# POOL issues the gathers of a group in two parts, with a wait for the first part's landing between them

## The reference: what is computed

```
h = relu(layernorm(x))
Q, K, V = h@Wq+bq, h@Wk+bk, h@Wv+bv                  # 8 heads of 16
scores = sum(Q[dst]*K[src], -1)*scale + edge@We + be
p = exp(scores - segment_max[dst]) / segment_sum[dst]
x = x + segment_sum(p * V[src], dst) @ Wo + bo        # layer 0
h = logmap0(relu(layernorm(x))) @ W.T + b
x = x + expmap0(segment_sum(h[src]*dinv[src]*dinv[dst], dst))   # layer 1
```

## Time and profile before

| | |
|---|---|
| median of 3 runs | 1495.47 us |
| the profiled execution | 1495.77 us |
| its span, first to last instruction | 1493.8 us |
| mean granted TensorE clock | 0.678 of full speed |
| busy: PE, DVE, ACT, POOL | 946.3, 740.5, 391.2, 595.5 us |
| gathers of the first loop (L662) | 416, mean 953 ns |
| gathers of the second loop (L695) | 208, mean 955 ns |

### The profile page before, as it was taken

One profiled execution on the slowest core, in us unless ns is written; L12 is line 12 of the kernel. 1 busy time (PEld: TensorE's weight loads), 2 busy tenths in 40 slices (PEclk: granted clock), 3 DMA queues, 4 the chain that ended last, 5 costly groups with the idle time before them and its releaser, 6 DMA issues.

```text
span 1493.8 us, 22198 instructions
## 1 busy us (share of the span) xinstructions
PE 946.3 (63%) x5820; PEld 805.1 (54%) x5820; DVE 740.5 (50%) x2771; ACT 391.2 (26%) x1107; POOL 595.5 (40%) x629
## 2 busy tenths in 40 slices
PE   5355775775775775675675676733757756765775
PEld 2244664664664564564564565622656645654665
DVE  8344544544554554553553553583534544454454
ACT  1502212212212212211311311142323423432341
POOL 0544454354354354354354354005343443444341
PEclk9655566566566566566566566675867877877787
DMA  5622232232232232233232233012011111111111
GB/s 150 178 80 83 87 104 82 84 104 83 81 106 86 77 110 86 72 111 89 71 112 89 70 110 93 6 47 87 26 41 34 40 40 37 37 40 40 33 41 29
DMA packets 87848, 111.23 MB, mean 74 GB/s; under 512 B 20787, under 2 KB 65791, under 8 KB 87807
## 3 DMA queue, kind: packets, MB, share of 16 engines
q0 software_dynamic: 26624, 68.20, 15.8%
q1 hardware_dynamic: 61191, 42.64, 9.9%
HBM read 99.83 MB, written 10.95 MB: 74 GB/s over the span
## 4 chain that ended last, share of the span: by engine, by line
PE 33%; DVE 24%; issue 20%; another core or an unknown queue 19%; DVEq 2%; DMA 1%; SPq 0%; ACT 0%
PE ps_q L1547 10%; PE ps_q L1673 3%; PE ps_q L1698 3%; PE ps_s L1673 3%; PE ps_c L1531 3%; DVE sc L933 2%; DVE wv L1275 2%; PE ps_f L1601 2%; PE ps_f L1600 1%; DVE fwd_reset L1274 1%; DVE prod L927 1%; PE ps_c L1527 1%; DVE oh_lo L897 1%; PE ps_b L1673 1%
## 5 line engine op out<-in xcount | busy, mean ns | idle before, releaser
L662 POOL DMA_INDIRECT kv<-kv_tab,idx x416 | 396.6, 953 | 533.8 <-DVE wv L1004 367.6
L695 POOL DMA_INDIRECT kv<-hs_tab,idx x208 | 198.6, 955 | 335.9 <-PE ps_q L1682 191.6
L1369 ACT ACTIVATE S<-iota,nloc 128x128 f32<-128x128 f32 x384 | 122.0, 389 | 636.1 <-remote 635.0
L1547 PE MATMUL ps_q<-qwin,ST 128*128 128x128 f32 x832 | 207.0, 432 | 19.5 <-DVE prod L927 10.5
L1547 PEld LDWEIGHTS ps_q<-qwin,ST 128*128 128x128 f32 x832 | 187.1, 331 | 20.8 <-DVE prod L927 10.8
L1580 PE MATMUL ps_f<-oh_lo,oh_hi 128*50 128x64 bf16 x416 | 83.4, 301 | 96.2 <-issue 96.0
L927 DVE TENSOR_TENSOR prod<-kv,ps_q 128x512 f32<-128x512 f32 (+1 forms) x128 | 74.6, 583 | 140.2 <-issue 58.8
L1011 DVE TENSOR_SCALAR fb<-ps_c 128x8 f32<-128x8 f32 x32 | 5.3, 166 | 274.3 <-remote 267.3
L1559 PE MATMUL ps_r<-wv,S 128*128 128x137 f32 x832 | 140.1, 341 | 1.8 <-DVE wv L1004 1.8
L1559 PEld LDWEIGHTS ps_r<-wv,S 128*128 128x128 f32 x832 | 140.0, 253 | 2.1 <-DVE wv L1004 2.1
L1580 PEld LDWEIGHTS ps_f<-oh_lo,oh_hi 128*50 128x50 bf16 x416 | 54.2, 172 | 110.4 <-issue 109.4
(11 more groups left out here) (257 smaller groups left out, 1715.6 us busy)
## 6 DMA issues: line engine op xcount, KB each, us to landing
dloc_b<-dloc_tab SPq DMA_DIRECT2D x32, 416.0 KB
kv<-kv_tab,idx POOLq DMA_INDIRECT x416
attr_s<-in_attr SPq DMA_DIRECT2D x32, 192.0 KB
kv<-hs_tab,idx POOLq DMA_INDIRECT x208
kv_tab<-qkv SPq DMA_DIRECT2D x5, 640.0 KB, 4.0
x_tab<-x SPq DMA_DIRECT2D x32, 64.5 KB, 1.7
qwin<-q_tab SPq DMA_DIRECT2D x32, 64.0 KB
xwin<-in_x SPq DMA_DIRECT2D x32, 64.0 KB
```

Source lines behind the costliest of these rows:

```text
L662: pool.indirect_dma_start(out=kv[:, b, t, :], out_offset=None, in_=kv_tab, in_offset=bass.IndirectOffsetOnAxis(ap=idx[:, b, t:t + 1], axis ...
L695: pool.indirect_dma_start(out=kv[:, j, t, 0:D], out_offset=None, in_=hs_tab, in_offset=bass.IndirectOffsetOnAxis(ap=idx[:, j, t:t + 1], ax ...
L1369: A.activation(S[:, b, t, :], iota[:], ACT.Abs, bias=nloc[:, g, t:t + 1] if known(g) else nloc[:, bass.ds(g, 1), t:t + 1].rearrange("p g t ...
L1547: mm = M.matmul(ps_q[c % 2][:, (t - t0) * D:(t - t0 + 1) * D], ST[:, b, t, :], qwin[:, b, :], start=True, stop=True)
```

## The change

A constant `HALF = 7` is added. Before it issues the eighth gather of a group (`t == HALF`), POOL waits for gathers of the same group. In the first loop it waits on the semaphore of chunk 1 until the gathers of tiles 4, 5 and 6 have landed (`16 * (t - t0)` = 48 above what the earlier groups in that buffer left). In the second it waits until seven gathers on `s_g1[j]` have landed (112 above). Then it issues the other six.

```diff
+HALF = 7
...
                     for t in range(t0, t1):
+                        if t == HALF:
+                            wait_apart(pool, s_kv[b][c], 32 * (g - b) + 16 * (t - t0), (s_tab[0], 32 * 3))
                         pool.indirect_dma_start(out=kv[:, b, t, :], out_offset=None, in_=kv_tab,
...
                 for t in range(T):
+                    if t == HALF:
+                        wait_apart(pool, s_g1[j], 8 * T * (n - j) + 16 * t, (s_tab[0], 32 * 3))
                     pool.indirect_dma_start(out=kv[:, j, t, 0:D], out_offset=None, in_=hs_tab,
```

## The result

On the chip of the first comparison the change makes the kernel faster: 1228.81 us, the median of 4 runs (1227.59 to 1230.84), against 1495.45 us (1494.24 to 1497.34, 4 runs) before. The ratio is 0.8218, with a 95% interval of 0.8206 to 0.8231. The forecast was 1250 us. The profiled execution took 1227.9 us, of which 1225.7 is the span.

What follows compares the result with a forecast made beforehand. Bound: PE's completions held back while a burst of gathers runs. First loop 189, second loop 42 and heads 15 us sum to 246; 1495.8 - 246 gives about 1250 us, 1155 to 1320 for this case, stated range 1150 to 1420.

Steps and rivals of the forecast that it cites:

- What bounds the kernel: Both loops: gathers following one another delay PE's completions, from 6 to 10 us after a burst's first until it landed.
- The pause: POOL before each group's eighth gather: waiting for the landing takes 3 us, hidden while a period is over 19 us.
- First loop: L1011 released 7.6 us earlier, 1.3 lost again: 6.3 us a step, 30 steps, 189 us (bounds 228 and 111).
- the second burst's delay: First loop, the six gathers after the pause: completions may be delayed again up to 3.9 us; 1.3 us taken.
- Heads: Start of each loop, two groups gathered without a gap: last release sooner, 4.5 us each, together 15 us (0 to 25).
- Second loop: PE freed at the seventh gather's landing: 6.3, 2.7 us or nothing a pair; 3 taken, 14 pairs, 42 us (0 to 88).
- Blocks again at once: Rival, chance 0.20: second burst delays at once; first loop keeps about half, second gains nothing, about 1390 us.
- Nothing is freed: Rival, chance 0.14: the delay ends only when the thirteenth gather landed; 44 pauses of 3 us add 132 us, 1628 us.
- The delay only coincides with gathers: Rival, chance 0.05: something that gathers don't cause makes the delay; POOL's idle time takes in the pause, no change, 1495.5 us.

Runs made afterwards that it cites:

- the run without a pause on chip 9: The change with both added waits set on counts reached long before, so POOL does not stop, against the kernel before: 1508.74 us against 1510.69.

## Why the prediction was right, and what it did not see

**What bounds the kernel: right where it was read.** A delay of PE's completions while gathers follow one another, which a pause for a landing shortens, is what the traces with and without a pause show, on the first chip and on chip 9, and the run without a pause on chip 9 rules the instructions out. The conclusion was too narrow in one thing and too strict in another: DVE's completions are delayed too, and in the second loop some come through before the burst has landed. Nor is it shown that it is the landing, and not the stop, that frees them. The rule set against it in the prediction, *the Trainium skill's ("SBUF — State Buffer", "Who interferes with whom") that PE and ACT wait on nobody*, would not have foretold the traces of the chips with the delay, where PE idles 1.05 us and more between matmuls beside gathers, and agrees with chips 5 and 7. That section is about ports; whether a port has any part in the delay no run shows. The other, *issue a DMA early and wait for it late ("DMA: Bandwidth & Descriptors", "Rules for kernel authors")*, is right on chip 5 by 42 us and wrong on chip 9 by 244.

**The pause: 3 us taken, 2.5 and 2.3 us measured**, within the bounds 1.5 and 3.5. POOL resumes later than DVE by 0.9 us in the first loop, near the 1 us that was added for it.

**First loop: 189 us forecast, 213.8 measured** (from the first `weigh` to the last, 864.9 before and 651.1 after). The mis-sized term is the second burst's delay. It was put at 1.3 us a step, to make a period of 21.9; the period is 20.8 to 20.9. POOL has no idle time left, so six gathers of one group and seven of the next run on without a wait, and the delay does return (L1016 up to 2.0 us after L1572, not 0.42). But the pause then comes once every 20.9 us and ends 1.3 to 3.0 us behind L1572's start, in all steps but the first, so that little can be held back. One gather of each such run is also held up by `weigh` (2.31 us from 400.52); whether that break helps as well no run shows. (The working has the second burst end at 427.4 us; its own terms give 427.2, which changes nothing.) POOL's idle of about 2 us between groups was not there on the first chip (0.30 us); on chip 9 it is 1.3 to 2.5 us in 20 waits and 4.5 to 9.0 in five. There the loop gains 194.9 us (871.0 against 676.1), near the 189.

**Heads: 4.5 us forecast for the first, 15.6 measured** (first `weigh` at 97.4 before, 81.8 after). The estimate counted one release, moved from the twenty-sixth gather to the twentieth. The trace before also had a first wait of 9.00 us there, ahead of the 11.95 of the earlier trace rows, and both went. The rows shown left out the first of the two.

**Second loop: 42 us and a part of the heads (10.5) forecast, 38.8 measured** from the first gather to the end (477.2 against 438.4); on chip 9 it is 41.9 (484.1 against 442.2). The working was right in its times: throttled 5.7 us after the first gather, free at the seventh's landing, throttled again in the second burst. Taken apart, the head gives 8.8 us (first L1698 50.4 us after the first gather before, 41.6 after), the 14 pairs 31.6, or 2.3 a pair where 3 were taken, and the last stretch loses 1.6. That 3 came so near is partly luck: the working gave 6.3, 2.7 or nothing, according to where the delay falls, and 3 was chosen among them. The second pause shows what was behind it: 4.8 us a pair more (67.2 us over 14, on chip 9).

The terms give 213.8 + 15.6 + 38.8 = 268.2 us; the profiled executions differ by 267.9 (1495.77 - 1227.9). The forecast was 246. The prediction was read from a chip with the delay and measured on one; on chip 5 it would have had the sign wrong.

**The rivals.** "Blocks again at once" fell: the second burst leaves 5 us free. "Nothing is freed" fell: L1016 starts before the eighth gather. Its price, one pause times the number of groups for a loop that POOL bounds, came true on chips 5 and 7 in the second loop, 35 us. But its reason was another: on these chips there was nothing to free. "The delay only coincides with gathers" fell on the chips with the delay, since a pause among the gathers moves it.

**What was not seen** is that the delay does not come with the kernel alone. It was there on three chips and not on two, in every run of each visit. The prediction took the earlier trace rows as the behaviour of Trainium2. None of the views that it read told otherwise, but there was one hint: the releaser "another core or an unknown queue" for an engine of the same core. What makes two chips free of it and three not is open, and so is whether they stay so. The runs show no more than that the kernel, its order and the pace of the gathers are the same.

## What to carry to other kernels

Where an engine's wait for another ends on no known releaser while gathers run, look whether the releases fall on landings; if so, break the row of gathers with a wait for a landing; in the second loop a break after every four or five gathers did better than one in the middle. To place it just behind the completion on which most depends is an inference from the traces, and no run with the delay tested it. Measure such a change on several chips, with the kernel before beside it on each: here it is worth 16 to 18% on the two chips with the delay on which it was run (20% with a second pause in the second loop) and costs 4% on one without the delay. No version tried is best on both kinds of chip: with the delay it is the one with two pauses, without it the kernel before. And read before you add a pause how much the issuing engine idles a period: on chips 5 and 7 it cost little up to that idle time and nearly its full length beyond it.

## What the runs showed of the hardware that was not expected

- **Two kinds of chip, or of occasion.** The same kernel takes 1043 us on two chips and 1495 to 1511 us on three. On the slower ones completions of PE and DVE are held back, in the pairs shown from 5 to 6 us after the first gather of a burst: L1567's until 2.3 to 2.9 us after the last gather's end, others for 0.6 to 3.4 us. On the faster ones DVE follows 0.42 us after PE's L1572 starts, with gathers all around.
- **In the second loop the delay does not depend on the bytes of a row**: 4 and 512 bytes give 1505.93 and 1508.31 us, one run each.
- **POOL's wait for the landing of gathers takes 2.5 us for 1 KB rows and 2.3 us for 512 byte rows**, from the end of the last issue, on both kinds of chip. At the very first pause it is 4.6 us.
- **A gather issued beside `weigh` is held up until `weigh` ends.** Timeline of the change on chip 5:

```profile
432.00 2.79 POOL L665 DMA_INDIRECT kv<-kv_tab,idx  x1 [0.30 <-issue]
432.02 1.94 DVE L1009 TENSOR_TENSOR wv<-kv,wv 128x1024 f32<-128x1024 f32 x2
```

*The Trainium skill ("SBUF — State Buffer", "Who interferes with whom") says that a DVE instruction with two SBUF inputs contends with a GpSimd instruction that reads SBUF; by these rows the trace agrees.* The gather that starts 0.02 us before `weigh` takes 2.79 us in place of 0.95 and ends 0.83 us after `weigh` (434.79 against 433.96): it did its work once `weigh` was over. On the first chip the kernel before avoids this, because POOL starts a group only after `weigh`; the pause shifts the gathers into it there and on chip 5 (on chip 9 only 3 of them). It is not `weigh` alone: of the 62 gathers over 1.4 us in the first chip's trace of the change, 30 run beside `weigh` and 32 beside DVE's L877, a tensor_scalar, and those beside L877 are long on chip 5 without a pause too (32 of 35). On the first chip the mean of a gather rises from 953 to 1119 ns so, 69 us in all (465.6 - 396.6), which POOL's former idle time covers there.
